# Steps ahead of VectorE's own drive, element-wise work moved from VectorE to ScalarE, and the experts' kernels mixed by TensorE

## The reference

```
layer 0: rw = softmax(mlp(mean(x)))                      # 4 shares per image
         h  = silu(bn(exp_w @ x))                        # 96 -> 576 channels
         h  = silu(bn(dwconv5x5(h, sum_e rw[e] dw_w[e])))# kernels mixed per image
         h  = h * sigmoid(mlp(mean(h)))
         x  = x + bn((sum_e rw[e] pw_w[e]) @ h)          # 576 -> 96
layer 1: state-space block on group-normed x: in-projection, 3x3 depthwise conv, silu,
         delta = softplus(...), and for each of 4*192 channels and 16 states
         h_t = exp(delta_t A) h_{t-1} + delta_t u_t B_t ;  y_t = sum_n h_t C_t
         then LayerNorm, gate silu(z), out-projection, residual
layer 2: LayerNorm -> Fourier mixing (as products with cos/sin matrices) -> residual
         LayerNorm -> feed-forward: q = fp8e5 rounding, y = fp16(q(x) @ q(W)), fp16(y + q(b)), relu, again
layer 3: LayerNorm -> linear attention (no softmax) -> residual; LayerNorm -> feed-forward
```

## Time and profile before

| | before |
|---|---|
| median of 3 runs | 26279.49 us |
| profiled execution, its own time | 26389.19 us |
| its span, first to last instruction | 26387.5 us |
| busy, share of the span: VectorE | 24513.9 us, 93% |
| TensorE (matmul) | 20581.9 us, 78% |
| ScalarE | 11550.1 us, 44% |
| GpSimd | 8808.6 us, 33% |
| mean granted TensorE clock | 0.819 |
| DMA share | 0.2 |

### The profile page before, as it was taken

One profiled execution on the slowest core, in us unless ns is written; L12 is line 12 of the kernel. 1 busy time (PEld: TensorE's weight loads), 2 busy tenths in 40 slices (PEclk: granted clock), 3 DMA queues, 4 the chain that ended last, 5 costly groups with the idle time before them and its releaser, 6 DMA issues.

```text
span 26387.5 us, 375604 instructions
## 1 busy us (share of the span) xinstructions
PE 20581.9 (78%) x125002; PEld 8812.8 (33%) x125002; DVE 24513.9 (93%) x23378; ACT 11550.1 (44%) x15421; POOL 8808.6 (33%) x4999
## 2 busy tenths in 40 slices
PE   6778778787787787877877878778778787787786
PEld 2333333333333333333333333333333333333332
DVE  5999999999999999999999999999999999999998
ACT  2444444444444444444444444444444444444443
POOL 2333333333333333333333333333333333333331
PEclk8878888888788888887888878888888788888886
DMA  2222222222222222222222222222222222222222
GB/s 74 66 71 67 68 72 62 72 69 64 71 67 68 71 62 72 69 64 71 67 67 72 62 71 70 64 71 67 67 72 62 71 69 65 71 67 67 72 62 61
DMA packets 646792, 1791.26 MB, mean 68 GB/s; under 512 B 76999, under 2 KB 87059, under 8 KB 644760
## 3 DMA queue, kind: packets, MB, share of 16 engines
q1 hardware_dynamic: 624280, 1726.94, 22.6%
q10 hardware_dynamic: 20480, 38.29, 0.5%
HBM read 1707.39 MB, written 44.96 MB: 66 GB/s over the span
## 4 chain that ended last, share of the span: by engine, by line
DVE 37%; issue 34%; PE 20%; ACT 5%; DVEq 2%; POOL 1%; DMA 0%; SPq 0%; ACTq 0%; POOLq 0%
DVE prod L1064 15%; PE bank L457 11%; DVE state L1233 9%; PE pair L457 6%; DVE drive L1064 5%; PE scan_sum L457 4%; DVE work L1064 2%; ACT work L825 1%; POOL drive L1467 1%; DVE delta L1064 1%; ACT decay L825 1%; ACT L825 1%; DVE work L1308 1%; DVE work L1332 1%; DVE pwm L1153 1%
## 5 line engine op out<-in xcount | busy, mean ns | idle before, releaser
L1467 POOL TENSOR_TENSOR drive<-du,Bb 128x784 f32<-128x784 f32 x3072 | 5964.3, 1941 | 14627.3 <-DVE drive L1064 14627.3
L457 PE MATMUL scan_sum<-prod,fold 64*64 64x392 f32 x40960 | 6452.5, 594 | 2647.4 <-DVE prod L1064 2644.8
L457 PE MATMUL bank<-pad,dg 64*64 64x392 f32 x59008 | 7515.6, 501 | 222.5 <-ACT pad L825 149.0
L825 ACT ACTIVATE decay_even<-delta,alog 128x784 f32<-128x784 f32 x3072 | 2817.9, 917 | 10807.9 <-DVE state L1233 10764.1
L1064 DVE TENSOR_TENSOR prod<-state,Cb 128x784 f32<-128x784 f32 x6144 | 6245.0, 1016 | 0.0
L1233 DVE TENSOR_TENSOR_SCAN state<-decay,drive 128x784 f32<-128x784 f32 x3072 | 5771.6, 1879 | 243.3 <-DVE pwm L1153 11.8
L1233 DVE TENSOR_TENSOR_SCAN state<-decay_even,drive 128x784 f32<-128x784 f32 x3072 | 5484.7, 1785 | 151.8 <-ACT decay_even L825 83.6
L457 PEld LDWEIGHTS bank<-pad,dg 64*64 64x64 f32 x59008 | 3410.3, 141 | 3883.7 <-issue 3103.2
L457 PEld LDWEIGHTS scan_sum<-prod,fold 64*64 64x64 f32 x40960 | 1746.3, 151 | 6143.1 <-issue 3819.4
L1064 DVE TENSOR_TENSOR drive<-du,Bb 128x784 f32<-128x784 f32 x3072 | 3006.6, 979 | 116.5 <-issue 116.5
L1410 POOL TENSOR_SCALAR_AFFINE_SELECT dg<-kern 128x640 f32<-128x640 f32 x1600 | 2542.7, 1593 | 1674.6 <-PE bank L457 1389.9
(11 more groups left out here) (176 smaller groups left out, 17363.3 us busy)
## 6 DMA issues: line engine op xcount, KB each, us to landing
Bb<-bc_rows SPq DMA_DIRECT2D x2048, 392.0 KB, 3.6
Cb<-bc_rows SPq DMA_DIRECT2D x2048, 392.0 KB, 4.2
xin<-in_x SPq DMA_DIRECT2D x64, 294.0 KB, 4.3
x_kept<-xin ACTq DMA_DIRECT2D x64, 294.0 KB, 4.6
x<-x_kept SPq DMA_DIRECT2D x64, 294.0 KB, 3.9
out_dram<-t SPq DMA_DIRECT2D x64, 294.0 KB, 2.7
crossed<-pwm ACTq DMA_DIRECT2D x128, 96.0 KB, 2.1
delta<-in_x SPq DMA_DIRECT2D x8, 1176.0 KB, 7.6
```

The source lines that it names most:

```text
L457: return pe.matmul(out, lhsT, rhs, start=start, stop=stop)
L825: return act.activation(out, in_, f, bias=bias, scale=scale, **more)
L1467: pool.tensor_tensor(drive[:, j % 2, :], du[:, m, :], Bb[:, q % SLOTS, :], ALU.mult).then_inc(drive_r.sem, 1)
```

## The change

- VectorE runs the steps due after an odd unit **before** its drive of the next unit, not behind it.
- `go_on` merges the two lists by due time on every engine; before, all due steps of the tail came first.
- The mixing leaves VectorE: ScalarE writes the identity times each share into `share` (4 tiles of 128x128), TensorE sums `share[e] @ dww[e]` and `share[e] @ pww[e]` in PSUM (8 matmuls of 125 or 480 columns), ScalarE copies the two sums out.
- `norm`: TensorE multiplies by `less96`, the identity minus 1/C, so that the centred input comes out of PSUM; ScalarE copies and squares it.
- `ffn`: both biases (and the maximum with 0) move to ScalarE. `pre`: `xn1` moves to ScalarE.
- The tail's due times (TAIL_AT) change, mostly to 3 units earlier in the middle; GpSimd's first two diagonals are due at 4.0 and not at 2.0.

```diff
-TAIL_AT = ((0, 9.8), (6, 20.0), (11, 24.8), (16, 29.6), (20, 39.5), (21, 41.0), (25, 47.5), (32, 53.5),
+TAIL_AT = ((0, 9.8), (6, 17.0), (11, 21.8), (16, 26.8), (20, 36.8), (21, 38.3), (25, 44.5), (32, 50.5), (40, 58.0), (42, 60.0),
...
-    for s in steps:
-        while s.at <= at:
-            s.next()
+    while steps and min(s.at for s in steps) <= at:
+        min(steps, key=lambda s: s.at).next()
...
 TensorE, expand and head
-                    if later(i):
-                        pe.wait_ge(dl_a.sem, dl_a.at(i - 1))
+                    pe.wait_ge(kern_r.sem, kern_r.at(i))
...
-                yield LEAD_AT - 1
+                yield LEAD_AT - 2
+                pe.wait_ge(share_r.sem, share_r.at(i))
+                if later(i):
+                    pe.wait_ge(dl_a.sem, dl_a.at(i - 1))
+                for out, stack in ((P[0][:, 0:T0 * TAPS], dww), (P[1][:, 0:T0 * C], pww)):
+                    for e in range(E):
+                        last = mm(out, share[:, e, :], stack[:, e, :], start=e == 0, stop=e == E - 1)
+                last.then_inc(mix_mm.sem, 1)
+                yield LEAD_AT - 0.6
                 expand(i, 0)
...
 TensorE, norm
-                    mm(T[h][0:C, 0:HALF], mean96[:, :], t2[:, h * HALF:(h + 1) * HALF]).then_inc(lm.sem, 1)
+                    mm(T[h][0:C, 0:HALF], less96[:, :], t2[:, h * HALF:(h + 1) * HALF]).then_inc(lm.sem, 1)
...
 ScalarE
+            def shares(i):
+                yield 0.0
+                act.wait_ge(rwc_r.sem, rwc_r.at(i))
+                for e in range(E):
+                    ac(share[:, e, :], ident[:, :], ACT.Copy, scale=rwc[:, e:e + 1]).then_inc(share_r.sem, 1)
...
             def head(i):
+                yield LEAD_AT - 1
+                act.wait_ge(mix_mm.sem, mix_mm.at(i))
+                ac(kern[:, :], P[0][:, 0:T0 * TAPS], ACT.Copy).then_inc(kern_r.sem, 1)
+                ac(pwm[:, :], P[1][:, 0:T0 * C], ACT.Copy).then_inc(kern_r.sem, 1)
...
+                yield GATE_AT + 10.6
+                act.wait_ge(g_sh.sem, g_sh.at(i))
+                ac(xn1, xin[:, :], ACT.Identity, bias=gst[:, 7:8], scale=gst[:, 6:7]).then_inc(xn1_r.sem, 1)
...
-                    act.wait_ge(lc.sem, lc.at(i, 2 * n + h + 1))
-                    ac(w[1][0:C, cols[h]], w[0][0:C, cols[h]], ACT.Square).then_inc(lq.sem, 1)
+                    act.wait_ge(lm.sem, lm.at(i, 2 * n + h + 1))
+                    ac(w[0][0:C, cols[h]], T[h][0:C, 0:HALF], ACT.Copy)
+                    ac(w[1][0:C, cols[h]], T[h][0:C, 0:HALF], ACT.Square).then_inc(lq.sem, 1)
...
-                        ac(h16[:, m, h * HALF:(h + 1) * HALF], T[h][:, 0:HALF], ACT.Copy).then_inc(h_16.sem, 1)
+                        t = h16[:, m, h * HALF:(h + 1) * HALF]
+                        ac(t, T[h][:, 0:HALF], ACT.Copy).then_inc(h_16.sem, 1)
+                        act.wait_ge(h_16.sem, h_16.at(i, q))
+                        ac(t, t, ACT.Relu, bias=ffn_b1[f][:, m:m + 1]).then_inc(h_b.sem, 1)
...
 VectorE, scan
+                    go_on(between, j)
                     if j % 2 == 1 and j + 1 < NU:
                         driving(j + 1)
-                    go_on(between, j)
...
-                v.tensor_scalar(xn1, xin[:, :], gst[:, 6:7], gst[:, 7:8], ALU.mult, ALU.add).then_inc(xn1_r.sem, 1)
-                    tt(w[0][0:C, cols], t2[:, cols], T[h][0:C, 0:HALF], ALU.subtract).then_inc(lc.sem, 1)
-                        v.tensor_scalar(t, t, ffn_b1[f][:, m:m + 1], 0.0, ALU.add, ALU.max).then_inc(h_b.sem, 1)
-                    link(v.tensor_scalar(o16[:, cols], o16[:, cols], ffn_b2[f][:, :], None, ALU.add))
```

More of the change, by code:

```diff
@@ L40 @@
 SETUP_LINKS = 53
-LEAD_LINKS = 14
-TAIL_LINKS = 6
+LEAD_LINKS = 5
+TAIL_LINKS = 2
 DVE_LINKS = LEAD_LINKS + TAIL_LINKS
@@ L157, in build @@
         mean96 = sb("mean96", [C, C])
+        less96 = sb("less96", [C, C])
         mean192 = sb("mean192", [128, 128])
@@ L213, in build @@
         rwc = sb("rwc", [128, E])
+        share = sb("share", [128, E, 128])
         kern = sb("kern", [128, T0 * TAPS])
@@ L271, in build @@
         rw_c = sig("rw_current")
-        kern_r, pwm_r = sig("kernels_mixed"), sig("pointwise_mixed")
+        rwc_r, share_r, mix_mm, kern_r = sig("shares_read"), sig("shares_spread", E), sig("experts_mm"), sig("kernels_mixed", 2)
         diag_r, diag_u = sig("diagonals_built", GROUPS), sig("diagonals_used", 21)
@@ L1018, in ffn @@
                     act.wait_ge(o_mm.sem, o_mm.at(i, 2 * f + h + 1))
-                    ac(o16[:, h * HALF:(h + 1) * HALF], T[h][0:C, 0:HALF], ACT.Copy).then_inc(o_16.sem, 1)
+                    t = o16[:, h * HALF:(h + 1) * HALF]
+                    ac(t, T[h][0:C, 0:HALF], ACT.Copy).then_inc(o_16.sem, 1)
+                    act.wait_ge(o_16.sem, o_16.at(i, 2 * f + h + 1))
+                    ac(t, t, ACT.Identity, bias=ffn_b2[f][:, :]).then_inc(o_b.sem, 1)
             def attention(i):
@@ L1040, in ahead @@
             def ahead(i):
+                yield from shares(i + 1)
                 yield from softplus(i, 4, NK, 0.4, 1.6)
                 yield from lead(i + 1)
+            go_on([Beside(shares(0))], END)
             go_on([Beside(lead(0))], END)
@@ L1081, in _ @@
             v.wait_ge(s_par.sem, PARAMS)
+            v.tensor_scalar(less96[:, :], ident[0:C, 0:C], -1.0 / C, None, ALU.add)
             v.tensor_copy(rT2b[:, :, :], rT2[:, :].unsqueeze(2).to_broadcast([RHID, E, 128]))
@@ L1134, in mix @@
             def mix(i):
-                link(v.tensor_copy(rwc[:, :], rw[:, i, :] if isinstance(i, int) else
-                                   rw[:, bass.ds(i, 1), :].rearrange("p b e -> p (b e)")))
-                if later(i):
-                    v.wait_ge(dw_d.sem, dw_d.at(i, 0))
-                if later(i):
-                    v.wait_ge(pw_d.sem, pw_d.at(i, 0))
-                link(v.tensor_scalar(kern[:, :], dww[:, 0, :], rwc[:, 0:1], None, ALU.mult))
-                for e in range(1, E):
-                    ins = v.scalar_tensor_tensor(kern[:, :], dww[:, e, :], rwc[:, e:e + 1], kern[:, :], ALU.mult, ALU.add)
-                    if e < E - 1:
-                        link(ins)
-                ins.then_inc(kern_r.sem, 1)
+                v.tensor_copy(rwc[:, :], rw[:, i, :] if isinstance(i, int) else
+                              rw[:, bass.ds(i, 1), :].rearrange("p b e -> p (b e)")).then_inc(rwc_r.sem, 1)
             def head(i):
-                yield LEAD_AT + 4
-                link(v.tensor_scalar(pwm[:, :], pww[:, 0, :], rwc[:, 0:1], None, ALU.mult))
-                for e in range(1, E):
-                    link(v.scalar_tensor_tensor(pwm[:, :], pww[:, e, :], rwc[:, e:e + 1], pwm[:, :], ALU.mult, ALU.add))
                 yield GATE_AT + 2.4
@@ L1264, in norm @@
             def norm(i, at, n, out, **more):
-                yield tail_at(at + 1)
-                for h in range(2):
-                    cols = slice(h * HALF, (h + 1) * HALF)
-                    v.wait_ge(lm.sem, lm.at(i, 2 * n + h + 1))
-                    tt(w[0][0:C, cols], t2[:, cols], T[h][0:C, 0:HALF], ALU.subtract).then_inc(lc.sem, 1)
                 yield tail_at(at + 5)
                 v.wait_ge(lr.sem, lr.at(i, 2 * n + 2))
-                v.wait_ge(lc.sem, lc.at(i, 2 * n + 2))
                 alone()
@@ L1385, in ahead @@
             def ahead(i):
-                yield 0.6
+                yield -0.5
                 mix(i + 1)
@@ L1423, in lead @@
                     if q < DRING:
-                        yield LEAD_AT - 2
+                        yield LEAD_AT
                     elif q < CONV3:
```

15 lines of the change are left out of this document (7 added, 8 removed).

## The result

The changed kernel takes 26328.23 us (median of 15 runs, 26319.76 to 26338.13) against 26270.64 (15 runs) for the kernel before: ratio 1.0022, 95% interval 1.0014 to 1.0030. The forecast was 25100. VectorE did get the lighter program that the prediction describes, and nearly all of it turned into waiting.

The account below looks back on a forecast made before the run. VectorE was taken to set the pace nearly everywhere, TensorE close behind. Terms 16.8 + 10.7 + 4.7 - 13.9 = 18.3 us a period, over 62 periods plus about 45, less 109.7 carried over, gave 25100; range 24550 to 25700.

Parts of the forecast that it names:

- (b): Casts before unit 93 wait for a bias ScalarE makes behind unit 94's even decay: 2.0 us a period added, bounds 0 and 2.5.
- (c): x1 step of unit 64 loses the three steps that covered the pointwise product: 1.5 us a period added, bounds 0 and 3.
- in full: VectorE sets the pace nearly everywhere; work taken off it, 16.8 us a period, counts in full where TensorE is not next.
- the collisions: VectorE's steps no longer run beside GpSimd's drive, losing their excess price: 10.7 us a period gained, bounds 5 and 11.6.
- (d): Gains given back where TensorE is next, around units 66 to 80 and the middle: 3.8 us a period, bounds 0 and 12.
- the first delta: VectorE's wait for the first delta goes, since ScalarE takes delta's work ahead of the norm's: 2.0 us a period gained.
- (a): TensorE's mixing in front of the LayerNorm's mean of squares delays the scale: 6.6 us a period added, bounds 4.3 and 11.2.
- rival 1: Mixing at the scan's start is hidden, its wait of 6.6 us a period absent: 24690 us, chance 18%.
- rival 2: TensorE becomes the bound of the middle and mixing runs at the lower clock throughout: 25755 us, chance 14%.
- Rival 3: GpSimd's drive or diagonals still collide with VectorE, 10.7 us a period not gained: 25775 us, chance 8%.
- Rival 4: Mixing's wait breaks TensorE's stream, the middle's clock falls to 0.74, slower than before: 27800 us, chance 4%.
- The carry-over: Median of the runs taken to lie 109.7 us below the profiled execution, as before: 25209 becomes 25100.

Follow-up runs that it names:

- e6: The changed kernel with the old table of places and the mixing on VectorE; new order, merged lists and moves to ScalarE stay: 25584.43 us, ratio 0.9720.
- e3: The changed kernel with the table of places of the kernel before; mixing stays on TensorE in front of the mean: 25815.90 us, ratio 0.9812.
- e9: The changed kernel with one VectorE step, the scaling of the tail's first LayerNorm, two units later: 25984.88 us, ratio 0.9873.
- e10: The changed kernel with two of five taps of the depthwise convolution's first four tiles left out on TensorE: 26079.25 us, ratio 0.9908.
- e1: The kernel before with only VectorE's steps of an odd unit put in front of its own drive: 25997.03 us, ratio 0.9879.
- e12: The changed kernel with mixing behind the mean of squares, old places, and VectorE's fold moved from scan 26 to 28: 25654.26 us, ratio 0.9757.
- e5: The kernel before with only the work moved from VectorE to ScalarE, centring in TensorE's matmul; old order, places and mixing: 25789.02 us, ratio 0.9802.
- e4: The changed kernel with VectorE's drive in front of the steps again: 26954.91 us, ratio 1.0243.

## Why the prediction was wrong, point by point

The differences of the runs put the parts into one sum, here in us a period (a run's difference divided by 62) beside the prediction's terms for the same part:

| part | forecast | measured |
|---|---|---|
| order, merged lists and moves (e6) | -11.9 - 10.7 - 2.0 + 3.8 = -20.8 | -718: -11.6 |
| mixing on TensorE (e6 to e3) | +6.6 - 4.9 = +1.7 | +228: +3.7 |
| new places (e3 to the changed kernel) | -2.7 + 2.0 + 1.5 = +0.8 | +547: +8.8 |
| sum | -18.3 | +57: +0.9 |

Another sequence of undoing gives other shares (the table alone costs 335 to 547), but in this one two steps failed, of about the same size, and the mixing by a little.

- **First failed step: the new places, 8.0 missed.** The prediction counted the table as a gain of 2.7 a period for attention's products against 2.0 at the casts (b) and 1.5 at unit 64 (c). These three held: 2.9, 1.9 and 2.4 from e3 to the changed kernel. It never asked, for each other step that the table puts earlier, where the result that it waits for stands in ScalarE's and TensorE's own programs, nor which units get more of TensorE's work. The runs show 547/62 = 8.8 a period lost, the greater part at a single step (e9), and units 40 to 47 longer by 3.8.
- **Second failed step: "in full" for VectorE's time, 9.2 missed.** The prices were right: 11.9 of durations for the moves (10.2 in the sum, with 1.7 of waits besides), 10.5 for the collisions (10.7; that casts suffer shows in their mean of 594 and not in rows 5, where the cast takes 0.37). The time they bought was 513/62 = 8.3 and 309/62 = 5.0, and with the merged lists 718/62 = 11.6, where 22.6 less the 3.8 of (d) and 2.0 more for the first delta were forecast. By the traces, from before to e6, durations fell by 20.4, waits rose by 5.2 where the terms had them unchanged, and 2.9 went into lost overlap, which the prediction did not have. The merged lists it put at nothing but the first delta's gain, and e6 has the 5.84 and 3.91 of units 78 and 26. Why the moves and the order alone give back part of what they save, 1.7 and 2.1 of waits, is argued and not shown: the other engines' work stands at fixed units, so VectorE would reach the same waits sooner.
- **(a) the mixing's wait** was right in mechanism and size: 1.4 to 8.7, thus 7.4 against 6.6, inside its bounds 4.3 to 11.2. So rival 1 is out. Net of VectorE's 4.9 the part should have cost 1.7 and cost 3.7.
- **(b)** casts in front of scan 93: 1.92 against 2.0. **(c)** x1 at unit 64: 2.99 against 1.5, at its upper bound of 3. **The first delta's wait** went, 1.96 to 0.
- **(d) TensorE next**: 3.8 was the value. e10 shows a bound in units 40 to 47 alone, worth at least 3.4, and the table lengthened that stretch. So rival 2 holds for eight units and not for the middle, though its sign (middle above 185, VectorE waiting for TensorE) came true. That sign did not tell a bound from a place.
- **Rival 3** is out: `du` has one price. The Trainium skill's rule ("SBUF — State Buffer", Who interferes with whom), as the prediction used it, lets all 11.6 go and has diagonals block too. In e1 the five groups of the sum lost 11.9, while the products and odd scans got 1.6 longer and one other step now meets a diagonal (950 to 1496 ns), as L1316 does in the changed kernel. **Rival 4** is out: the clock of the middle is 0.93, of 0.94.
- **The carry-over.** Before, the profiled execution lay 109.7 over the median, and the sum took that off. The profiled execution of the changed kernel lies at its median (span 26325.9). That is 110 of the 1228 us missed. By the traces, which compare profiled executions, the period explains 17.6 x 62 = 1091 (the runs, above, give 19.2 a period): 14.2 of waits, 2.7 of overlap, 0.7 of durations. The rest, 27, is the ends' part.

Left open: what the merged lists are worth alone, through what else than the casts the value of the order depends on the places, and how the table's remaining 163 us divide over the other moved places. None of these was tried alone.

## What to carry to other kernels

When a change moves steps to earlier places in an in-order program, list for each the instruction that feeds it and what stands ahead of that one on its own engine; steps placed too early cost 547 us here, three quarters of the 718 that order, moves and merged lists had gained. Move a waiting step only if the next link of its chain has room behind it: e9 gained 384 us and e12 lost 229 by the same kind of edit. Put new work of another engine behind the link that the critical engine waits for, not in front: one number here was worth 480 us. A new rule for ties between two lists is a change of every engine's program: list what it reorders.

## What the runs showed of the hardware

- A scan on VectorE started 0.07 us before the end of an unrelated step and 0.04 after that of the drive it reads and waits for; over a period of 96 scans the lost overlap is 1.8 (e5 to e6) to 2.5 us (e1).
- The place of the mixing sets its clock: 7.1 us after 3.09 us of idleness, 4.3 behind work. The spectrum's matmuls show the same, 4.26 behind 3.76 us of idleness (clock 0.65) against 2.84 (1.00), and so does the expansion in front of unit 17, 2.98 us behind 4.80 (0.50) against 1.58 at the scan's start (1.00). A wait thus lengthens what comes behind it.
- A cast of 128x392 to fp8 costs 358 to 365 ns where GpSimd does not hold it up. Beside GpSimd's drive it took 1762 (126 casts of the kernel before) and 1999 (315 casts of e4).
